# Joining the two halves of the mixed values inside the cross stage instead of the rows stage

## The reference, cut to what matters

```python
# x: (32, 100, 512), ctx: (32, 722, 512); 16 heads of 32
q = layernorm(x) @ wq + bq;  k = ctx @ wk + bk;  v = ctx @ wv + bv      # by head
attn = softmax(q k^T) v                                                # 100 x 722 a head
x1 = x + tanh(g_xattn) * (attn @ wo + bo)
# then a second, masked self-attention block on layernorm(x1), over 100 rows a batch
```

## Time and profile before

| | us |
|---|---|
| median of 3 runs (2612.43 to 2616.61) | 2613.17 |
| profiled execution | 2608.9 |
| its span | 2607.1 |
| cross stage | about 111 to 1898 |
| rows stage | about 1900 to 2257 |

### The profile page before, as it was taken

The page is one execution under the profiler, slowest core; times in us unless marked ns, Lnnn a source line. Parts: engine busy times, 40 slices in busy tenths (PEclk is TensorE's granted clock), DMA queues, the critical chain, the costliest instruction groups (busy, mean ns, idle before and its releaser), DMA issues. The chain is left out here.

```text
span 2607.1 us, 47776 instructions
## 1 busy us (share of the span) xinstructions
PE 2504.7 (96%) x17376; PEld 2271.7 (87%) x17376; DVE 1804.5 (69%) x2869; ACT 1332.0 (51%) x3000; POOL 384.0 (15%) x281
## 2 busy tenths in 40 slices
PE   7899999999999999999999999999969999699999
PEld 6889999999999999999999999999848888588887
DVE  7467777777777777777777777777757666456665
ACT  3344555555555545555555555455534444355554
POOL 0311111111111111111111111111124333000000
PEclk9999999999999999999999999999869999789999
DMA  7645545555545555455554555544469999899993
GB/s 224 204 119 134 124 124 128 128 132 127 130 122 129 131 129 135 113 130 130 131 128 121 127 131 128 128 130 116 108 165 209 207 202 197 184 180 189 188 184 82
DMA packets 324830, 379.91 MB, mean 146 GB/s; under 512 B 126332, under 2 KB 232220, under 8 KB 324636
## 3 DMA queue, kind: packets, MB, share of 16 engines
q1 hardware_dynamic: 322772, 375.80, 61.4%
q10 hardware_dynamic: 1864, 1.43, 0.2%
HBM read 162.57 MB, written 72.57 MB: 90 GB/s over the span
## 5 line engine op out<-in xcount | busy, mean ns | idle before, releaser
L740 DVE TENSOR_TENSOR c_parted<-c_prob,c_parted 128x600 fp32r<-128x600 f32 x512 | 400.7, 783 | 363.3 <-ACT c_prob L686 363.3
L864 PE MATMUL c_mix<-c_parted,c_v 120*66 120x200 f32 (+1 forms) x3072 | 544.7, 270 | 0.7 <-DVE c_parted L740 0.6
L849 PEld LDWEIGHTS c_pair<-c_q_stack,c_k_stack 100*120 100x120 f32 (+1 forms) x3072 | 517.5, 186 | 10.9 <-issue 6.3
L849 PE MATMUL c_pair<-c_q_stack,c_k_stack 100*120 100x100 f32 (+1 forms) x3072 | 519.9, 227 | 6.3 <-DVE c_parted L740 5.0
L726 DVE TENSOR_REDUCE c_peak<-c_pair 100x1 f32<-100x724 f32 x512 | 456.6, 907 | 55.2 <-PE c_pair L811 39.8
L682 ACT ACTIVATE c_parted<-c_pair 128x600 fp32r<-128x600 f32 x512 | 344.4, 673 | 283.6 <-PE c_pair L849 283.4
L864 PEld LDWEIGHTS c_mix<-c_parted,c_v 120*66 120x66 f32 (+1 forms) x3072 | 418.2, 140 | 3.1 <-DVE c_parted L740 0.9
L686 ACT ACTIVATE c_prob<-c_pair 128x600 f32<-128x600 f32 x512 | 341.8, 668 | 0.0
L664 ACT ACTIVATE c_v<-c_work 120x512 fp32r<-120x512 f32 (+1 forms) x192 | 115.6, 602 | 442.4 <-PE c_work L91 442.4
L811 PE MATMUL c_pair<-c_k_stack,c_q_stack 96*100 96x362 f32 x1024 | 254.2, 329 | 0.0
L1657 ACT ACTIVATE s_prob<-s_scores,s_shift 106x100 f32<-106x100 f32 x512 | 169.6, 363 | 136.1 <-DVE s_shift L1690 136.1
(11 more groups left out here) (200 smaller groups left out, 5296.1 us busy)
## 6 DMA issues: line engine op xcount, KB each, us to landing
c_k_stack<-c_k_hi SPq DMA_DIRECT2D x1024, 90.2 KB, 2.1
e_stage<-in_ctx SPq DMA_DIRECT2D x32, 1444.0 KB, 6.4
c_k_stack<-c_k_lo SPq DMA_DIRECT2D x512, 90.2 KB, 2.1
c_q_stack<-q_parts SPq DMA_DIRECT2D x192, 100.0 KB, 2.4
mix_parts<-w_mixed SPq DMA_DIRECT2D x64, 200.0 KB, 3.2
r_parts<-mix_parts SPq DMA_DIRECT2D x22, 512.0 KB, 7.5
s_q_stack<-qk_parts SPq DMA_DIRECT2D x10, 800.0 KB
s_k_stack<-qk_parts SPq DMA_DIRECT2D x10, 800.0 KB
```

Source lines behind the costliest of these rows:

```text
L740: dve.tensor_tensor(p[:, :, 1, :], prob[i % 2][:], p[:, :, 0, :], ALU.subtract).then_inc(p_lo_done, 1)
L849: return pe.matmul(pair[i % 2][0:r, t // (CT // 2), col:col + S], k_stack[:, i, c_cols(t)], q_stack[:, i, :], start=True, stop=True)
L864: return pe.matmul(mix[g % 2][0:VW, at * 2 * S:(at + 1) * 2 * S], v[0:r, t, i, :], parted[i % PR][0:r, t, :, :].rearrange("p a s -> p (a s)"),
```

## The change

In the cross stage the reduction of a group becomes two: one takes rows 32 to 63 of the PSUM bank into `low`, a new tile of 32 partitions with four buffers, and the old one takes all 66 rows into `mixed`. GpSimd then adds `low` to the first 32 rows of `mixed`. The next use of a `low` buffer waits for the join four groups before, TensorE waits for both reductions before it reuses the bank, and the store of a batch waits for the last join. One store goes to `mix_dram` instead of two to `mix_parts`, and the rows stage loads one part and does one sum less.

```diff
@@ stage_cross, SyncE
             def store_mix(b):
                 sp.wait_ge(mixed_done, (b + 1) * (H // HG))
-                for n in range(2):
-                    dst = mix_parts[n].rearrange("(h d) n -> d h n", d=HD)[:, :, bass.ds(b * S, S)]
-                    sp.dma_start(dst, mixed[n * HD:(n + 1) * HD, :, :]).then_inc(stored, 16)
+                sp.wait_ge(joined, (b + 1) * (H // HG))
+                dst = mix_dram.rearrange("(h d) n -> d h n", d=HD)[:, :, bass.ds(b * S, S)]
+                sp.dma_start(dst, mixed[0:HD, :, :]).then_inc(stored, 16)
@@ stage_cross, GpSimd
+            def join(b, g):
+
+                pool.wait_ge(low_done, b * (H // HG) + g + 1)
+                pool.wait_ge(mixed_done, b * (H // HG) + g + 1)
+                high = mixed[0:HD, g * HG:(g + 1) * HG, :]
+                pool.tensor_tensor(high, high, low[g % LOWS][:], ALU.add).then_inc(joined, 1)
+
+            def join_all(b):
+                for g in range(H // HG):
+                    join(b, g)
+
             with pool.Fori(0, B // 2 - 1) as u:
                 split_columns(u * 2 + 1, 1)
+                join_all(u * 2)
                 split_columns(u * 2 + 2, 0)
+                join_all(u * 2 + 1)
...
@@ stage_cross, VectorE
                     if g == 0 and stored_before:
-                        dve.wait_ge(stored, b * 48)
-
-                    dve.tensor_reduce(mixed[:, g * HG:(g + 1) * HG, :],
-                                      mix[g % 2][0:VW, 0:HG * 2 * S].rearrange("p (h a s) -> p h s a", a=2, s=S),
-                                      AX.X, ALU.add).then_inc(mixed_done, 1)
+                        dve.wait_ge(stored, b * 32)
+                    use = b * (H // HG) + g
+                    if use >= LOWS:
+                        dve.wait_ge(joined, use - LOWS + 1)
+                    both = mix[g % 2][:, 0:HG * 2 * S].rearrange("p (h a s) -> p h s a", a=2, s=S)
+                    dve.tensor_reduce(low[g % LOWS][:], both[HD:2 * HD], AX.X, ALU.add).then_inc(low_done, 1)
+                    dve.tensor_reduce(mixed[:, g * HG:(g + 1) * HG, :], both[0:VW], AX.X, ALU.add).then_inc(mixed_done, 1)
@@ stage_cross, TensorE
                 if at == 0 and g >= 2:
+                    pe.wait_ge(low_done, b * (H // HG) + g - 1)
                     pe.wait_ge(mixed_done, b * (H // HG) + g - 1)
@@ stage_rows, SyncE
             def load_mix(buf, cols, rows, landed):
-                for n in range(2):
-                    src = mix_parts[n].rearrange("(k p) n -> p k n", p=P)[:, :, rows]
-                    sp.dma_start(parts[buf][:, n, :, cols], src).then_inc(landed, 16)
+                src = mix_dram.rearrange("(k p) n -> p k n", p=P)[:, :, rows]
+                sp.dma_start(parts[buf][:, 0, :, cols], src).then_inc(landed, 16)
@@ stage_rows, join_attn
-            step.done(engine.tensor_tensor(attn[:], parts[u % 2][:, 0, :, cols], parts[u % 2][:, 1, :, cols], ALU.add))
-            step.wait(engine)
-            engine.tensor_tensor(attn[:], attn[:], parts[u % 2][:, 2, :, cols], ALU.mult).then_inc(a_joined, 1)
+            engine.tensor_tensor(attn[:], parts[u % 2][:, 0, :, cols], parts[u % 2][:, 1, :, cols], ALU.mult).then_inc(a_joined, 1)
```

More of the change, by code:

```diff
@@ L419 @@
 HG = 2
+LOWS = 4
 PR = 3
@@ L490, in work_use, with stage_cross @@
     return (index, index) if b is None else (CT + index, A_FIRST + b * A_USES + CT + index)
-def stage_cross(nc, shared, cross_w, context, q_parts, mix_parts, prob_sums, inverses, wo, w_qkv):
+def stage_cross(nc, shared, cross_w, context, q_parts, mix_dram, prob_sums, inverses, wo, w_qkv):
     with ExitStack() as ctx:
@@ L509, in stage_cross @@
         mixed, sums = cross_w.mixed, cross_w.sums
+        low = [m.sb(f"low{i}", [HD, HG, S]) for i in range(LOWS)]
         work = [m.ps(f"work{i}", [P, 512]) for i in range(2)]
@@ L525, in stage_cross @@
         p_lo_done, mix_done = m.sem("p_lo_done"), m.sem("mix_done")
-        mixed_done, stored = m.sem("mixed_done"), cross_w.mix_stored
-        sums_in, sums_done = m.sem("sums_in"), m.sem("sums_done")
+        mixed_done, joined, stored = m.sem("mixed_done"), m.sem("joined"), cross_w.mix_stored
+        sums_in, sums_done, low_done = m.sem("sums_in"), m.sem("sums_done"), m.sem("low_done")
         block = ctx.enter_context(nc.Block())
@@ L596, in _ @@
             body(B - 2, False)
-            sp.wait_ge(stored, 48 * EARLY * 4)
+            sp.wait_ge(stored, 32 * EARLY * 4)
             for a in range(EARLY):
@@ L626, in _ @@
             pool.wait_ge(cleared, 3)
+            def join(b, g):
[6 more added lines that the diff above has]
+                    join(b, g)
             with pool.Fori(0, B // 2 - 1) as u:
                 split_columns(u * 2 + 1, 1)
+                join_all(u * 2)
                 split_columns(u * 2 + 2, 0)
+                join_all(u * 2 + 1)
             split_columns(B - 1, 1)
+            join_all(B - 2)
             pool.wait_ge(ct_lo_done, B * KT)
-            for n in range(2):
+            for n, joins in enumerate((range(LOWS - 1), range(LOWS - 1, H // HG))):
                 for k in range(KT):
@@ L636, in _ @@
                                        ALU.subtract).then_inc(cross_w.row_lo, 1)
+                for g in joins:
+                    join(B - 1, g)
         @block.scalar
@@ L949 @@
 PROJ_LOAD, STACK_LOAD = TILES - 5, TILES - 4
-A_LOADS = 2 + HPT
-A_STEPS = 2
+A_LOADS = 1 + HPT
+A_STEPS = 1
 PAIRED = (TILES + 1) // 2
@@ L955, with stage_rows @@
 SIM_STEPS = 6
-def stage_rows(nc, shared, cross_w, begin, x, mix_parts, prob_sums, inverses, bv, g_xattn, bo, g_info, w_qkv, g_ffn, b_proj, x1_dram,
+def stage_rows(nc, shared, cross_w, begin, x, mix_dram, prob_sums, inverses, bv, g_xattn, bo, g_info, w_qkv, g_ffn, b_proj, x1_dram,
                qk_parts, values_dram, sim_dram, table_dram, w_proj):
@@ L972, in stage_rows @@
         value_bias = m.sb("value_bias", [P, KT])
-        parts = [m.sb(f"parts{i}", [P, 3, KT, 2 * P]) for i in range(2)]
+        parts = [m.sb(f"parts{i}", [P, 2, KT, 2 * P]) for i in range(2)]
         last_sums = cross_w.sums[0:H, :]
@@ L1116, in _ @@
                 if t == 0:
-                    sp.wait_ge(cross_w.mix_stored, 48 * B)
+                    sp.wait_ge(cross_w.mix_stored, 32 * B)
                     sp.dma_start(last_sums, prob_sums[:, EARLY * BLOCK:ROWS]).then_inc(sums_in, 16)
@@ L1875, in flamingo_block @@
             stage_queries(nc, shared, cross_w, x, wq, bq, ident, q_parts, ctx_1024, wk, wv, bk, neg_ident)
-            stage_cross(nc, shared, cross_w, ctx_1024, q_parts, mix_parts, prob_sums, inverses, wo, w_qkv)
+            stage_cross(nc, shared, cross_w, ctx_1024, q_parts, mix_dram, prob_sums, inverses, wo, w_qkv)
         begin = SelfStart(nc, ctx, cross_w.mixed)
-        stage_rows(nc, shared, cross_w, begin, x_rows, mix_parts, prob_sums, inverses, bv, g_xattn, bo, g_info, w_qkv,
+        stage_rows(nc, shared, cross_w, begin, x_rows, mix_dram, prob_sums, inverses, bv, g_xattn, bo, g_info, w_qkv,
                    g_ffn, b_proj, x1, qk_parts, values, sim, tables, w_proj)
```

6 lines of the change are left out of this document (3 added, 3 removed).

## The result

The changed kernel takes 2642.27 us (median of 4 runs, 2640.04 to 2649.86) against 2614.55 us (median of 4 runs, 2612.43 to 2616.61) for the kernel before: a ratio of 1.0111, 95% interval 1.0088 to 1.0134. It is slower, as forecast, but by some 28 us and not by 9.5; the time lies outside the range that ended at 2636. The profiled execution took 2640.04 us, its span is 2638.2 us against 2607.1.

A forecast was written before the change was run, and what follows sets the result against it. TensorE was taken as full in both stages, so only late L740 results cost: 31 batches at 0.30 (9.3), last batch +1.5, seam -1.3, sum +9.5 us; forecast 2622.7 us, range 2611 to 2636.

The forecast's parts named there:

- What bounds the kernel: Both stages: TensorE is full, so relieving GpSimd, VectorE or queues gains nothing; added VectorE work costs only if TensorE waits.
- The room of 0.16 and 0.45 us: Cross stage: how much later L740 may end before TensorE loses time, 0.16 us at place A, 0.45 at place B.
- the 0.06 of early loading: Cross stage: unhindered, TensorE makes a step's first weight load some 0.06 us before it is needed.
- The price of the new reduction: VectorE, cross stage: the second reduction costs what the present one does, 0.56 us long, 0.49 from start to next start.
- place A: Cross stage, L740 of heads 6, 8, 10: 0.19 later against 0.16 of room, 0.03 us each, two of three counted.
- place B: Cross stage, L740 of heads 4 and 12, reduction and key residual before it: 0.49 later, 0.45 room, 0.04 us.
- Which steps are late: Cross stage, per batch: two of three steps at place A (heads 6, 8, 10), both at place B (heads 4, 12).
- The join at B: Cross stage, place B: GpSimd's join of 0.59 us holds L740 from 1009.12 to 1009.22, making the step 0.15 late.
- Second rival: Cross stage: L740 held back more by a later, longer or longer-holding join; 0.6 to 0.9 a batch, about 2635; chance 0.22.
- Last batch: Last cross batch: third join before four weight splits, back to back, holds an L740 up to 1.2 us once or twice: +1.5.
- Seam: Between last batch and rows stage: last store +0.7, one load and one sum less -2.0, together -1.3 us.
- other waits: Cross stage: waits for bank reuse, joins and the batch's store cost nothing; late key copies taken as 0, 3 us allowed.

The follow-up runs named there:

- the third experiment: Changed kernel with the low reduction reading rows 0 to 31 of the bank instead of 32 to 63 (result not the sum of the halves): 2625.53 us.
- The second experiment: Changed kernel without the low reduction; GpSimd's joins stay and add a tile of zeros: 2629.66 us, batch period 55.16.
- the first experiment: Changed kernel without GpSimd's joins, both reductions kept and nobody waiting for a join: 2638.26 us, batch period 55.60.
- the fourth experiment: Changed kernel with all joins of the last batch placed behind the weight splits on GpSimd: 2637.38 us, last batch 35.92.
- seventh experiment: Changed kernel, nothing left out, with the low reduction moved ahead of L740 into VectorE's idle time: 2618.42 us, batch period 54.85.
- sixth: Changed kernel without the low reduction, each join also waiting until the L740 behind its group is done: 2623.99 us, batch period 54.85.

## Why the prediction was wrong

**What bounds the kernel: right.** Work taken from GpSimd (POOL from 39 to 29 in the earlier trace rows's second stretch) and from the queues gave nothing, and what counted in the cross stage was how late L740 comes. The room of 0.16 and 0.45 us was right too, the 0.06 of early loading included: the steps behind a late one are 0.06 shorter than before (1.935 against 1.995), which is the part of the delay that TensorE doesn't lose.

**The price of the new reduction: this step failed.** "VectorE's time goes by elements a partition in every row here, so I take the price of the present one", 0.49 from its start to the next. The elements were right (0.57 us long against 0.56), the spacing wasn't: 0.71, for the reason of the third experiment. Put into the prediction's own sums, place A is 0.19 + 0.22 - 0.16 = 0.25 late instead of 0.03, place B 0.49 + 0.22 - 0.45 = 0.26 instead of 0.04. The rows that I had taken from before held no instruction of another group of partitions with its neighbours close by. Its trace did, in the front part of a batch, on the output's side: L731 writes rows 96 to 99 of `q_stack`, L726 writes from row 0.

```profile
1030.34 0.90 DVE L726 TENSOR_REDUCE c_peak<-c_pair 100x1 f32<-100x724 f32 x1
1031.27 0.57 DVE L731 TENSOR_TENSOR c_q_stack<-c_mix,f_neg_ident 4x400 fp32r<-4x400 f32 x1
1031.87 1.73 DVE L726 TENSOR_REDUCE c_peak<-c_pair 100x1 f32<-100x724 f32 x2
```

Each starts 0.03 after the recorded end of the one before it, where the instructions of the earlier trace rows overlap; so do 96 of the 96 L726 that follow an L731. That was a sign of such a spacing before the change was tried. And I bounded the price from below only ("nothing") and took the upper end to be the old instruction itself. With rooms used up to a hundredth, an upper bound was the one that mattered.

**Which steps are late: half right.** Head 4 has before it a reduction and a key residual, but also 0.22 us of idleness, and its step has A's room and not B's; I had it with B. In the changed kernel the steps that wait for heads 4, 8 and 12 come 0.31 or 0.32 later each, net of the early loading 0.25 to 0.26; those for heads 6 and 10 wait as well but lose nothing more (0.05 later, 0.05 regained), since L740 of heads 5 and 9 did not come later with the step before and leaves them more room: L759 of head 9 starts 1.59 after that of head 8, at 1014.27, where it was 1.99. Three times 0.25 is 0.75, measured 0.74. The prediction had said that a late step gives room to the next and counted two of three at A; only head 8 of the three loses time.

**The join at B: wrong in the changed kernel, right as a mechanism.** "L740, ready at 1009.12, goes at 1009.22", 0.1 us late on account of the join. The join's length was right (0.60 for 0.59); it starts 0.14 after the recorded end of the old reduction (1019.99 and 1020.14 before head 12) where the prediction took 0.08. The second experiment's join, which waits for one of the two reductions instead of both, has the 0.08. But the low reduction itself keeps VectorE so busy that L740 stands ready before the join begins, and then it goes first. Apart from head 14 (0.98, where there is room for it) joins held L740 only without the low reduction (1.10), or where it cost less or was moved (0.97), by the amount that the prediction's release would give: 1009.58 + 0.61 - 0.14 + 0.78 = 1010.83 is the end of that L761. What the Trainium skill says ("SBUF — State Buffer", section "SBUF: two separate sides"), that the one that starts first keeps the ports, doesn't hold for the recorded starts: by it the join at 1005.17 should have held the L759 at 1005.45.

**Second rival.** It gave 0.6 to 0.9 a batch and some 2635, the period that came, at a chance of 0.22. But its mechanism was a longer or longer-holding join, and the first experiment excludes it; its other leg, no early loading, is excluded by the 0.06 above. The right period was luck for this rival.

**Last batch: mis-sized.** The prediction saw the splits come back to back and took "up to 1.2 us once or twice", the length of one split. Four in a row held one L740 for all their time, 5 us: VectorE didn't get in between them. The term is +5.2 by the fourth experiment instead of +1.5. The other 2.5 us go with the clock's earlier fall, which the prediction didn't have and which no trace ties to the change.

**Seam, other waits, rows stage: right, the seam in part by luck.** The seam gave -1.5 for -1.3. Its parts were less well sized: the store starts 2.0 us after the last mix matmul instead of 0.6, twice the +0.7 of the sum; from there to VectorE's first sum it is 9.2 instead of 11.4 (-2.2 for -1.3); and from that sum to TensorE's first product 3.0 instead of 3.7, for the one sum less (L1160 and L1162 are two, where there were three of 0.69). The new waits cost nothing, since the period is the same without the one for the join in the first experiment; and the rows stage's sums gave no gain.

**The two terms together.** With 0.71 for 0.49, with one late step at A and two at heads 4 and 12, and with 5.2 for the last batch the working gives 31 x 0.76 + 5.2 - 1.3 = 27.5 us. The medians are 27.7 apart, but that is closer than it deserves. The count of the late steps was read from the trace of the changed kernel; with the prediction's own count, two at A and two at B, and its 0.06 for the earlier stalls, it would be 31 x 0.96 + 5.2 - 1.3, some 34 us. And the two profiled executions are 31.1 apart, with 2.5 that go with the clock and 3.2 at the end whose cause is open.

## What to carry to other kernels

Where an engine's result is wanted within tenths of a microsecond, price an added instruction by its spacing with those neighbours, not by its length: a VectorE instruction that reads PSUM from another group of 32 partitions cost 0.71 instead of 0.49 us between neighbours that read from the first. Look in the trace of before for such neighbours in other stages, too. Look for an idle slot of the same engine first: the same instruction placed there cost nothing. And don't let GpSimd have several instructions with SBUF operands ready in a row beside a VectorE instruction on the critical path that has two: here they were harmless as long as each waited for its own releaser.

## What the runs showed of the hardware that I had not expected

- A change of the starting partition of a PSUM input (0, 32, 0) keeps the instruction and the one behind it each until 0.03 us after the predecessor's end, 255 and 256 times of 256; with the start at 0 they overlap. VectorE outputs that start at partition 96 and 0 in turn show the same 0.03 in the kernel before, 96 times of 96.
- Between VectorE and GpSimd it isn't the recorded start that decides. A sum of two SBUF tiles whose operands were ready 0.17 us before a GpSimd instruction began, but which was queued behind another VectorE instruction and started 0.28 after it, went first (0.77 us), and GpSimd waited (1.51). With operands ready 0.02 or 0.07 after GpSimd's start it waited itself (0.97, 0.98). In the traces of the changed kernel and of the second, third, fourth and seventh experiment, up to the last batch, this holds for every L740 that starts while a join runs, at least 0.15 us before its recorded end: ready 0.17 us or more before the join's start, it went first (155 cases); ready 0.01 or more after it, it waited (347).
- Four GpSimd instructions ready in a row kept one VectorE instruction for 4.2 to 5.1 us, in the changed kernel and in the second, third, sixth and seventh experiment: nothing let it in between them.
- Two delays that cost 0.74 and 0.30 us a batch alone cost 0.74 together.
